# Adding the residual by accumulating transfers instead of on VectorE, at the end of a sandwich-norm transformer layer

## What is computed

```python
x = x + layernorm(attn(layernorm(x), wq, wk, wv, wo))       # 32 heads, 8 kv heads, rope
x = x + layernorm(ffn(layernorm(x), up, down, up_scale, down_scale, output_scale))

# ffn(h):  hidden = relu((h @ sign(up).T) * up_scale)       # 2048 -> 8192
#          out    = (hidden @ sign(down).T) * down_scale * output_scale   # 8192 -> 2048
```

## Time and profile before

| | us |
|---|---|
| three runs | 2292.95, 2441.72, 2475.57 |
| their median | 2441.72 |
| the profiled execution's own time | 2310.72 |
| its span (slowest core, core 7) | 2309.2 |
| spans of the 8 cores in it | 2273.2 to 2309.2 |

### The profile page before, as it was taken

How to read it: one execution, slowest core, us unless ns; L and a number is a source line. 1 busy time by engine, 2 the same in 40 slices (tenths; PEclk the granted TensorE clock), 3 DMA queues, 4 the chain that set the end, 5 groups by cost and what they waited for, 6 DMA issues and landing times.

```text
span 2309.2 us, 40937 instructions; the slowest of 8 cores (2273.2 to 2309.2 us)
## 1 busy us (share of the span) xinstructions
PE 2214.3 (96%) x15744; PEld 1229.6 (53%) x15744; DVE 908.5 (39%) x1689; ACT 1484.8 (64%) x1443; POOL 58.6 (3%) x99
## 2 busy tenths in 40 slices
PE   4999899999999999999989899999999999999996
PEld 2555467776677765655556544444444444444442
DVE  4777433434344434442453644211221122112167
ACT  5765599999999999999999943322222222222224
POOL 1000100000000000000000100000000000000000
PEclk9888999999999999999999999999999999999998
DMA  9965232221122010017544755644333334444453
GB/s 265 253 230 191 70 64 71 81 81 30 51 81 80 13 20 1 2 19 130 87 105 74 162 186 178 231 163 149 146 146 146 146 146 148 162 160 166 163 223 146
DMA packets 59597, 286.61 MB, mean 124 GB/s; under 512 B 14352, under 2 KB 14352, under 8 KB 35728
## 3 DMA queue, kind: packets, MB, share of 16 engines
q1 hardware_dynamic: 47520, 246.70, 30.1%
q0 software_dynamic: 10704, 36.87, 9.7%
q10 hardware_dynamic: 1184, 0.43, 0.1%
HBM read 290.29 MB, written 29.36 MB: 138 GB/s over the span
## 4 chain that ended last, share of the span: by engine, by line
PE 88%; DVE 3%; ACT 3%; DMA 3%; issue 2%; DVEq 0%; ACTq 0%; POOL 0%; SPq 0%
PE woP L62 38%; PE pv L542 19%; PE sc L62 11%; PE kvP L62 5%; PE fP L687 5%; PE fP L62 4%; PE qP L62 3%; ACT ex L526 2%; PE tpP L66 1%; DMA xb<-x 1%; DMA W<-wkv 1%; DMA xresF<-x 1%; DMA wstg<-wkv 1%; PE fP L66 0%; DMA wo<-wo 0%
## 5 line engine op out<-in xcount | busy, mean ns | idle before, releaser
L526 ACT ACTIVATE ex<-sc,ebias 128x1024 bf16<-128x1024 f32 x1024 | 1040.0, 1130 | 33.3 <-PE sc L62 30.1
L971 ACT ACTIVATE pan<-stg 128x2048 bf16<-128x2048 f32 x128 | 234.6, 1898 | 597.6 <-PE woP L62 577.1
L542 PE MATMUL pv<-ex,VT 128*128 128x256 bf16 x4096 | 537.4, 274 | 6.2 <-DVE nsA L555 4.9
L542 PEld LDWEIGHTS pv<-ex,VT 128*128 128x128 bf16 x4096 | 359.6, 98 | 151.6 <-issue 115.8
L62 PE MATMUL sc<-QT,KT 64*128 64x256 bf16 x4096 | 325.7, 272 | 21.4 <-ACT ex L526 20.1
L62 PEld LDWEIGHTS sc<-QT,KT 64*128 64x128 bf16 x4096 | 153.2, 94 | 197.8 <-issue 181.7
L62 PE MATMUL woP<-xn2Tb,pan 128*128 128x512 bf16 x1024 | 231.0, 379 | 1.1 <-DVE xn2Tb L1059 1.1
L62 PE MATMUL woP<-xn2Ta,pan 128*128 128x512 bf16 x1024 | 231.0, 379 | 1.1 <-DVE xn2Tb L1059 1.1
L62 PE MATMUL woP<-pan,hidb 128*128 128x512 bf16 x1024 | 223.5, 379 | 0.0
L62 PE MATMUL woP<-pan,hida 128*128 128x512 bf16 x1024 | 223.5, 379 | 0.0
L555 DVE COPY nsA<-pv 128x512 f32<-128x512 f32 x64 | 44.3, 692 | 415.0 <-PE pv L542 410.1
(11 more groups left out here) (107 smaller groups left out, 1550.9 us busy)
## 6 DMA issues: line engine op xcount, KB each, us to landing
stg<-upw SPq DMA_DIRECT2D x64, 1024.0 KB, 7.9
stg<-dnw SPq DMA_DIRECT2D x64, 1024.0 KB, 7.8
xb<-x SPq DMA_DIRECT2D x32, 1024.0 KB, 8.3
xnT_rl<-xsp SPq DMA_DIRECT2D x48, 512.0 KB, 3.3
wo<-wo POOLq DMA_DIRECT2D x48, 512.0 KB, 7.9
xsp<-xnT_rg SPq DMA_DIRECT2D x24, 512.0 KB, 5.8
out<-dacc SPq DMA_DIRECT2D x16, 512.0 KB, 2.9
wstg<-wkv SPq DMA_DIRECT2D x4, 1024.0 KB, 18.9
```

The costliest lines, as they stand in the source:

```text
L526: t_e[s] = p.s(lambda e: e.activation(ex[s % NE][:], sc[s % 3][:], AF.Exp, bias=ebias[:], scale=0.125))
L542: t_pv[s] = p.do("tensor", lambda e, o=o, r=r, c=c, first=first, last=last: e.matmul(pv[:, r * 256:(r + 1) * 256], VT[:, o:o + 128], ex[s ...
L971: t_sign[n, k] = p.s(lambda e: e.activation(pan[n % 2][:, k * 2048:(k + 1) * 2048], stg[sl][:], AF.Sign))
```

## The change

The tensor xr2sp is gone. The residual goes to the output tensor when it is made, by the same SyncE DMAs. All eight loads of the residual, the buffers xr_lo and the list rest are gone, and so is the addition on VectorE. Instead, as soon as ScalarE has normalised a half, GpSimd issues a DMA of that half, 128x1024 float32, that adds it to what stands in out. It waits for the normalisation and for the landing of the tile's residual write. The program ends when so and the three sp semaphores are complete.

```diff
@@ o_norm
-            t_sp[t] = p.dma("sync", xr2sp[t * 128:(t + 1) * 128, :], y[:], "sp2")
+            t_sp[t] = p.dma("sync", out[t * 128:(t + 1) * 128, :], y[:], "sp2")
@@ wo_ln
-            t_sp[t] = p.dma("sync", xr2sp[t * 128:(t + 1) * 128, :], xres[b][:], "sp%d" % b)
+            t_sp[t] = p.dma("sync", out[t * 128:(t + 1) * 128, :], xres[b][:], "sp%d" % b)
@@ last_ln
             for c in range(2):
...
-                rest.append((tt, c, t_no, xr_buf, t_res))
-
-        def add_out(tt, c, t_no, xr_buf, t_res):
-            dc = dacc[:, tt * 2048 + c * 1024:tt * 2048 + (c + 1) * 1024]
-            xc = xr_buf[:, c * 1024:(c + 1) * 1024]
-            p.wait("vector", t_no, t_res)
-            t_o = p.v(lambda e: e.tensor_add(dc, dc, xc))
-            p.wait("sync", t_o)
-            p.dma("sync", out[tt * 128:(tt + 1) * 128, c * 1024:(c + 1) * 1024], dc, "so")
+                p.wait("gpsimd", t_no, t_sp[tt])
+                p.do("gpsimd", lambda e, dc=dc, c=c: e.dma_start(
+                    out=out[tt * 128:(tt + 1) * 128, c * 1024:(c + 1) * 1024], in_=dc, accum_op=ALU.add), "so", 16)
@@ the FFN's loop
-            if qt == 3:
-                p.wait("sync", t_um)
-                for i in range(4):
-                    tt = 4 * (1 - U) + i
-                    xr_tok[tt] = p.dma("sync", xr_lo[i][:], xr2sp[tt * 128:(tt + 1) * 128, :], "xr%d" % i)
...
-                if n == 29:
-                    for i in range(4):
-                        tt = 4 * U + i
-                        p.wait("sync", stg_free[i])
-                        xr_tok[tt] = p.dma("sync", stg[i][:], xr2sp[tt * 128:(tt + 1) * 128, :], "sg%d" % i)
@@ block
-            while rest:
-                add_out(*rest.pop(0))
@@ the end
-        while rest:
-            add_out(*rest.pop(0))
-        p.wait("sync", p.now("so"))
+        p.wait("sync", p.now("so"), p.now("sp0"), p.now("sp1"), p.now("sp2"))
```

More of the change, by code:

```diff
@@ L105, in build_nc @@
     out = nc.dram_tensor("out", [1024, 2048], F32, kind="ExternalOutput")
-    xr2sp = nc.dram_tensor("xr2sp", [1024, 2048], F32, kind="Internal")
     xsp = nc.dram_tensor("xsp", [24 * 128, 2048], BF16, kind="Internal")
@@ L119, in build_nc @@
                   "wp1", "wp2", "wp3", "sg0", "sg1", "sg2", "sg3",
-                  "xr0", "xr1", "xr2", "xr3", "sp0", "sp1", "sp2", "so", "xs0", "xs1", "xs2", "rl0", "rl1",
+                  "sp0", "sp1", "sp2", "so", "xs0", "xs1", "xs2", "rl0", "rl1",
                   "cf0", "cf1", "cf2", "cf3"):
@@ L180, in build_nc @@
         sf_sb = at("sf_sb", Z + 176, 2048, F32)
-        xr_lo = [at(f"xr_lo{i}", Z + kb, 2048, F32) for i, kb in enumerate((32, 40, 96, 104))]
         bst8 = at("bst8", 1.0625, 8 * 24, F32)
@@ L1101, in build_nc @@
         t_bn = {}
-        xr_tok = {}
         hid_free = [None, None]
@@ L1157, in fold, with last_ln @@
                     bst8[:, tt * 24 + db * 6: tt * 24 + db * 6 + 6], dacc[:, lo:lo + 512]))
-        def last_ln(tt, xr_buf, t_res):
+        def last_ln(tt):
             o = tt * 8
@@ L1177, in last_ln @@
                                                          scale=mv8[:, o + 3:o + 4]))
-                rest.append((tt, c, t_no, xr_buf, t_res))
-        def add_out(tt, c, t_no, xr_buf, t_res):
-            dc = dacc[:, tt * 2048 + c * 1024:tt * 2048 + (c + 1) * 1024]
-            xc = xr_buf[:, c * 1024:(c + 1) * 1024]
-            p.wait("vector", t_no, t_res)
-            t_o = p.v(lambda e: e.tensor_add(dc, dc, xc))
-            p.wait("sync", t_o)
-            p.dma("sync", out[tt * 128:(tt + 1) * 128, c * 1024:(c + 1) * 1024], dc, "so")
+                p.wait("gpsimd", t_no, t_sp[tt])
+                p.do("gpsimd", lambda e, dc=dc, c=c: e.dma_start(
+                    out=out[tt * 128:(tt + 1) * 128, c * 1024:(c + 1) * 1024], in_=dc, accum_op=ALU.add), "so", 16)
         t_hid = {}
-        rest = []
         p.wait("tensor", *t_x2T[0:4])
@@ L1260, in build_nc @@
                 if n == 31:
-                    last_ln(i, xr_lo[i], xr_tok[i])
+                    last_ln(i)
         for i in range(4):
@@ L1264, in build_nc @@
             block(31, 1, i, (1, i))
-            last_ln(4 + i, stg[i], xr_tok[4 + i])
-        while rest:
-            add_out(*rest.pop(0))
-        p.wait("sync", p.now("so"))
+            last_ln(4 + i)
+        p.wait("sync", p.now("so"), p.now("sp0"), p.now("sp1"), p.now("sp2"))
         p.flush()
```

## The result

| us | before | after |
|---|---|---|
| median of nine runs each | 2294.18 | 2302.7 |
| lowest run | 2291.1 | 2298.91 |
| span of the profiled execution | 2309.2 (core 7) | 2297.7 (core 3) |
| span less the end of TensorE's last matmul, median of the 8 cores | 19.6 | 28.6 |

The ratio is 1.0034 with a 95% interval of 1.002 to 1.0047: 0.34% slower, about 8 us. The forecast was 4.8 us faster. Six more runs of the kernel before brought its median down from 2441.72 to 2294.18; two of the first three had been disturbed, and the ratio leaves such runs out.

What follows compares the result with a forecast made beforehand. TensorE bounds the kernel up to the last 19.6 us, where VectorE is behind; removing additions wins 10.1 us, halved by queued transfers to 4.8, so 2310.72 becomes 2305.9 us, said as 2306. Range 2283 to 2480.

Steps and rivals of the forecast that it cites:

- Its first half: End of the kernel: without VectorE's residual additions, the last result can be sent 10.1 us earlier.
- The backlog: After the last matmuls: VectorE's 16 residual additions, 18.8 us, make its last fold 8.8 us late; without them none is left.
- The residual's other place: Eight residual stores before the FFN's first panel, going to another HBM tensor: price 0, bounds -1 and +1 us.
- The queue: GpSimd's sixteen transfers from 2257.4 us on: they build a backlog, never run dry and set the end, 2304.4 us.
- The time T of an accumulation: Time on the DMA engines of each 512 KB adding transfer at the end: 2.84 us, bounds 1.35 and 7.9.
- the prediction's formula: End of the span: the later of 2258.95 + 16 T and 2298.15 + T, T being one accumulation's DMA engine time.
- The fixed part of 1.55 us: Part of a transfer's landing outside its DMA engine time, taken from a plain store: 1.55 us, bounds 0 and 5.1.
- The step that called GpSimd idle since 1320 us: GpSimd's queue before the final transfers: nothing done since 1320 us, so nothing queued behind or ahead of it.
- The issue on GpSimd: Issuing each final transfer: 0.53 us, 0.6 with the wait, only the first on the path; bounds 0.3 and 1.6.
- The forecast's bracket for T: Final transfers: 2.6 to 3.6 us of DMA engine time each, execution 2302 to 2318 us; chance 0.50.
- the rival of the slow queue: Final transfers from 2257 us: at 5.68 us each, end 40.6 us later; chance 0.21 for 3.6 to 6.03, 0.12 above.
- The prediction's own sign: Landings of the final transfers: growing from 4.4 us to some 13, falling to 8; 20 and more would mean slow transfers.

## Why the prediction was wrong

Its first half held, point by point. TensorE bounds all but the last 20 us. The backlog was VectorE's, made by the additions: in the changed kernel the last fold started 0.11 us after TensorE (predicted 0.16) and the last normalisation ended 6.4 us after it (6.4), and the run without additions gained 10.1 us (10.1). The residual's other place costs nothing, as said. The loads' removal wasn't run by itself; TensorE is as full as before in the windows after. The queue, as predicted, formed and did not run dry before the last transfer.

It was wrong in the end, a tail of 28.6 us where it gave 14.8 (19.6 - 4.8). Two steps failed, and together they turned a gain of 5 us into a loss of 8 to 9:

- **The time T of an accumulation**, set at 2.84 us by the nearest row, a conversion. The engines spent 3.5 to 3.8 us on one, 3.65 at the median of the cores after (and 3.2 to 3.9 in the kernels with eight of them). Packets overlap on an engine, so the end implies a little less. SyncE saw the last landing 24.0 us after TensorE at the median, where the prediction had 14.8, and 9.2 / 16 = 0.57 us more for each gives T = 3.42 (3.65 on the slowest core). In the prediction's formula, T = 3.14 was where the gain ends, so this step alone makes a loss of 4.4 us. The conversion was a poor neighbour: it has one source, and its target is in SBUF. The runs went 1.35 plain, 2.64 adding into SBUF, 3.65 adding into HBM. All of them had eight cores at work at once; what one core alone would take is not known.
- **The fixed part of 1.55 us**, taken from a store on SyncE's queue. It left out GpSimd's closing drain, which no step of the prediction named. The step that called GpSimd idle since 1320 us overlooked the drain's row. It ends 4.3 to 4.4 us after SyncE has seen the last semaphore in the changed kernel, 5.2 to 6.2 after plain stores and 5.0 to 5.8 with a lone 32 KB. Even with T = 2.84 the gain of 4.8 us would have shrunk to half a us or less, an estimate from these 4.3 us.

So of the 13.8 us by which the tail missed, the longer queue accounts for 9.2, the drain for 4.3 and the step from the drain's end to the span's end for the rest. The issue on GpSimd was longer too, 0.85 us in place of 0.53, and hardly on the path.

The forecast's bracket for T, 2.6 to 3.6, holds the 3.42; the rival of the slow queue (above 3.6) fits only the slowest core, and its price of +40 us at T = 5.68 was far too high. The prediction's own sign lay on this border: it wanted landings of at most some 13 us, and 20 and more for the slow queue. The longest were 18.3 to 19.0 us on four cores and 20.5 to 25.9 on the other four.

The 2302.7 us lie near the predicted 2306 only because the profiled execution of before, to which the gain was applied, was itself 16 us above the median of nine. That nearness is luck. The forecast was a change of -4.8, and the change was +8.

The sign that would have told was in the trace: a row of 17.15 us at the line that closes the program, on an engine that was called free because it had nothing more to do.

## What to carry to other kernels

Work taken off a late engine gains what its backlog was, but what replaces it must be priced by its own row; here an accumulating DMA into HBM took about 2.7 times a plain one (3.65 us for 512 KB against 1.35, medians of the cores). Don't let GpSimd's queue carry the last transfer of a program: its drain ended 4 to 6 us behind the last landing here, and cost nothing where the last transfer was early enough. Judge a tail on the core that sets the time: here the cores with the longest tails were not the slowest ones. Sharing the work worked best: four tiles by transfer, all issued before TensorE's end, and four on VectorE gave 0.9966 of the time before, where eight and none gave 1.0034 and 1.

## What the runs showed of the hardware that was not expected

- GpSimd's closing drain took 8.3 us after the issue of a single transfer of 32 KB that landed in 2.5 us, and 9.5 us after sixteen plain stores, each the same on all eight cores. Behind a long queue of accumulations it ended 4.3 to 4.4 us after the last landing (4.0 to 4.1 with transfers of 1 MB). SyncE's took 7 ns.
- An accumulation with its target in SBUF took the DMA engines 2.64 us on every core, twice a plain store to HBM (1.35 at the median); with its target in HBM 3.5 to 3.8, differing from core to core.
- The issue of an accumulation took GpSimd 0.85 us, that of a plain transfer 0.53.
